# All column transforms in two column tiles of 64, and a quarter of each mix operand copied by GpSimd between the pieces of its zeroing

## The reference

```python
x_ft = jnp.fft.rfftn(_gn(x), axes=(-2, -1))
blk  = jnp.einsum('bimn,hiomn->bhomn', x_ft[:, :, :32, :32], weight)      # 'mix'
xr   = jnp.fft.irfftn(zeros.at[:, :, :32, :32].set(blk), s=(64, 64))
x    = x + jnp.einsum('bchw,oc->bohw', xr, fc_w) + fc_b
g    = _gn(x)
att  = softmax(sigmoid(g.mean((2, 3)) @ ksm_w.T))
kern = clip(ifft2(einsum('bk,koihw->boihw', att, dft_weight)).real)
x    = x + (conv3x3(g, kern) + bias) * fbm_scale
```

## Time and profile before

| what | us |
|---|---|
| median of 3 runs (138.45, 139.57, 140.53) | 139.57 |
| span of the profiled execution | 137.8 |
| TensorE busy in it | 122.5 |
| VectorE, ScalarE, GpSimd busy | 87.8, 70.7, 52.8 |

### The profile page before, as it was taken

How to read it: one execution, slowest core, us unless ns; L and a number is a source line. 1 busy time by engine, 2 the same in 40 slices (tenths; PEclk the granted TensorE clock), 3 DMA queues, 4 the chain that set the end, 5 groups by cost and what they waited for, 6 DMA issues and landing times.

```text
span 137.8 us, 4822 instructions
## 1 busy us (share of the span) xinstructions
PE 122.5 (89%) x2060; PEld 91.8 (67%) x2060; DVE 87.8 (64%) x201; ACT 70.7 (51%) x143; POOL 52.8 (38%) x44
## 2 busy tenths in 40 slices
PE   0799997969997969979999979989999999999970
PEld 0799997869996959979999969873323432223230
DVE  0077696879996743553357685999873789922340
ACT  0468458538965336523317775644998329311100
POOL 7993000009999999999600550130500000000000
PEclk9999999999999999999999999999999999999997
DMA  3999999999500036787876899887989968884477
GB/s 90 268 272 257 233 222 357 302 384 399 204 5 7 0 81 156 171 203 165 181 164 153 172 178 153 180 202 164 168 184 175 211 156 189 195 191 105 104 162 143
DMA packets 71892, 25.17 MB, mean 183 GB/s; under 512 B 67904, under 2 KB 68160, under 8 KB 71872
## 3 DMA queue, kind: packets, MB, share of 16 engines
q1 hardware_dynamic: 70784, 24.62, 77.2%
q10 hardware_dynamic: 1088, 0.26, 0.9%
HBM read 14.38 MB, written 4.19 MB: 135 GB/s over the span
## 4 chain that ended last, share of the span: by engine, by line
PE 86%; issue 5%; DVE 3%; DMA 2%; ACT 0%; SPq 0%
PE slot L1050 27%; PE slot L882 14%; PE slot L963 11%; PE slot L978 8%; PE slot L941 6%; PE slot L952 5%; PE slot L908 3%; PE aggp L1008 3%; PE slot L904 3%; DMA x_buf<-x 2%; PE small L904 1%; PE aggp L904 1%; DVE kern L780 1%; PE aggp L941 1%; PE small L892 1%
## 5 line engine op out<-in xcount | busy, mean ns | idle before, releaser
L1050 PE MATMUL slot<-y_buf,conv_w 128*32 128x512 f32 (+1 forms) x136 | 31.7, 603 | 0.0
L1050 PE MATMUL slot<-w_buf,conv_w 128*32 128x512 f32 (+1 forms) x136 | 31.7, 603 | 0.0
L882 PE MATMUL slot<-cst,x_buf 128*64 128x64 f32 x512 | 19.0, 241 | 5.3 <-DMA x_buf<-x 4.5
L882 PEld LDWEIGHTS slot<-cst,x_buf 128*64 128x64 f32 x512 | 18.4, 154 | 5.6 <-issue 5.5
L821 DVE TENSOR_TENSOR bd_buf<-slot,q_buf 128x512 f32<-128x512 f32 (+1 forms) x17 | 11.0, 670 | 9.3 <-PE slot L1050 9.1
L1050 PEld LDWEIGHTS slot<-y_buf,conv_w 128*32 128x32 f32 x136 | 8.3, 109 | 12.6 <-issue 12.0
L441 POOL TENSOR_TENSOR x_buf<-y_buf 128x1024 f32<-128x1024 f32 x4 | 7.7, 1934 | 22.5 <-DVE y_buf L709 22.5
L978 PE MATMUL slot<-cst,t_buf 128*128 128x128 f32 x128 | 15.5, 278 | 0.8 <-issue 0.8
L978 PEld LDWEIGHTS slot<-cst,t_buf 128*128 128x128 f32 x128 | 14.7, 192 | 1.4 <-issue 1.2
L963 PE MATMUL slot<-cst,r_buf 128*64 128x128 f32 x256 | 14.6, 274 | 0.7 <-ACT r_buf L491 0.7
L613 DVE TENSOR_REDUCE row_sq<-q_buf 128x16 f32<-128x1024 f32 (+1 forms) x9 | 9.8, 1097 | 7.7 <-ACT q_buf L459 7.7
(11 more groups left out here) (128 smaller groups left out, 222.7 us busy)
## 6 DMA issues: line engine op xcount, KB each, us to landing
x_buf<-x SPq DMA_DIRECT2D x16, 256.0 KB, 4.3
w_buf<-w_modes SPq DMA_DIRECT2D x16, 256.0 KB, 5.0
x_buf<-x SPq DMA_DIRECT2D x32, 128.0 KB, 3.1
w_buf<-y_buf SPq DMA_DIRECT2D x16, 256.0 KB, 5.9
out<-bd_buf SPq DMA_DIRECT2D x28, 128.0 KB, 2.8
t_buf<-dft_w SPq DMA_DIRECT2D x4, 288.0 KB, 5.3
t_buf<-x_buf SPq DMA_DIRECT2D x8, 128.0 KB, 2.4
r_buf<-x_buf SPq DMA_DIRECT2D x8, 128.0 KB, 3.4
```

Source lines behind the costliest of these rows:

```text
L882: last = pe.matmul(ps[64 * ri:64 * ri + 64, col:col + 64], x_part(k)[:, i, q, :], const("fwd_h")[:, 64 * ri:64 * ri + 64], start=True, sto ...
L1050: last = pe.matmul(ps[32 * j:32 * j + 32, 32 * u0:32 * u1], cw[r][:, b, k, :], src, start=(k == terms[0][0]), stop=(k == terms[-1][0]))
```

## The change

Three edits. `f2` loses its path with 128 columns: k = 2 and 3 now use two column tiles of 64 like k = 0 and 1. `own_blocks` is gone: VectorE writes block 0 alone, ScalarE blocks 1 and 2. GpSimd copies block 3 from `zn[n]`, in a new function `last_block(n)`: the first before its late zeroing, the second and third between the two zeroings, the fourth between the two halves of the second zeroing, the others behind it and ahead of the 28 steps. `mix` waits for this on `bd_pool` too.

```diff
-        def own_blocks(n):
-            return (0, 1) if n % 2 else (0,)
@@ gpsimd
+            def last_block(n):
+                k, xx = divmod(n, 2)
+                gp.wait_ge(zn_ready, n + 1)
+                nc.gpsimd.tensor_copy(bd[k][96:128, 3, xx], zn[n][96:128]).then_inc(bd_pool, 1)
+                gp.wait_ge(bd_pool, n + 1)
+
+            last_block(0)
             gp.wait_ge(f1_done, 16)
             gp.wait_ge(sq_ready, 9)
             gp.wait_ge(bd_ready, 1)
             nc.gpsimd.memset(x_buf[:, 0:4096], 0.0).then_inc(bd_zero, 1)
             gp.wait_ge(bd_zero, 3)
-            nc.gpsimd.memset(x_buf[:, 4096:8192], 0.0).then_inc(bd_zero, 1)
+            last_block(1)
+            last_block(2)
+            nc.gpsimd.memset(x_buf[:, 4096:6144], 0.0).then_inc(bd_half, 1)
+            gp.wait_ge(bd_half, 1)
+            last_block(3)
+            nc.gpsimd.memset(x_buf[:, 6144:8192], 0.0).then_inc(bd_zero, 1)
             gp.wait_ge(bd_zero, 4)
+            for n in range(4, 8):
+                last_block(n)
@@ scalar, blocks(n)
-                for g in range(len(own_blocks(n)), 4):
+                for g in (1, 2):
@@ vector, operand(n)
-                for g in own_blocks(n):
-                    ps = slice(32 * g, 32 * g + 32)
-                    ins = nc.vector.tensor_tensor(bd[k][ps, g, xx], z[ps], rstd[ps], ALU.mult)
+                ins = nc.vector.tensor_tensor(bd[k][0:32, 0, xx], z[0:32], rstd[0:32], ALU.mult)
@@ tensor, f2_part
-                    if k >= 2:
-                        last = pe.matmul(ps[:, col:col + 64], y_rows[:, b, f:f + 4, :].rearrange("w g c -> w (g c)"),
-                                         const("fwd_w")[:, 0:64], start=True, stop=True)
-                        continue
                     for h in range(2):
                         last = pe.matmul(ps[64 * h:64 * h + 64, col:col + 64],
@@ tensor, mix
                 pe.wait_ge(bd_act, 2 * ml + xx + 1)
+                pe.wait_ge(bd_pool, 2 * ml + xx + 1)
```

More of the change, by code:

```diff
@@ L230, in spectral_then_attention_conv @@
         ones_ready = sem("ones_ready"); s_ready = sem("s_ready"); stat_read = sem("stat_read"); zn_ready = sem("zn_ready"); bd_act = sem("bd_act")
+        bd_pool = sem("bd_pool"); bd_half = sem("bd_half")
         bd_zero = sem("bd_zero"); w_zero = sem("w_zero"); pool = sem("pool_done"); taps_ready = sem("taps_ready")
```

## The result

| | before | changed |
|---|---|---|
| median, us (lowest to highest, runs) | 139.01 (138.01 to 140.61, 6) | 141.50 (140.26 to 142.62, 6) |
| span of the profiled execution, us | 137.8 | 139.6 |
| TensorE, GpSimd busy, us | 122.5, 52.8 | 120.5, 57.5 |

The changed kernel takes 1.0159 times as long, with a 95% interval of 1.0114 to 1.0205: 2.2 us more.

A forecast was written before the change was run, and what follows sets the result against it. The prediction took TensorE's instruction supply to bound the mix stretch: -3.3 us of work, all given back as longer holes, and +1.12 us for mix(3,1) behind the last hole, so 139.57 + 1.1 = 140.7 us, range 138.8 to 142.3.

The forecast's parts named there:

- What bounds the stretch: From 30.17 to 51.17 us, the supply of TensorE's instructions in blocks of 256 sets the pace, not its arithmetic.
- Work off TensorE is given back as holes: In the mix stretch, all 3.3 us of TensorE work saved return as longer holes while it waits for instructions.
- The blocks themselves come when they came before.: In the mix stretch, instruction blocks keep their times, the fifth again at 50.93 us: no loss from later blocks.
- TensorE's own work: In f2(2) and f2(3), matmuls in two column tiles of 64 take 3.3 us less TensorE work.
- GpSimd: Eight new copies of 32x512 at 1.0 us each delay the DFT steps but stay hidden, 0.95 us to spare at i1(3).
- the slower rival: GpSimd's copies and late DFT steps become the bound: 141.7 us at 1.6 us per copy; chance 15%.
- the faster one: In the mix stretch, blocks come early enough for the 3.3 us saving to be real: 138.4 us; chance 12%.
- The third rival: The fifth block comes a microsecond earlier and covers the extra mix(3,1), so time is unchanged at 139.6 us; chance 13%.
- The one term that was in the forecast: At the mix's end, all of mix(3,1) runs behind the last block end, adding 1.12 us.

The follow-up runs named there:

- e1: Kernel before with the transforms of f2(2) and f2(3) in two column tiles, nothing moved to GpSimd: 1.0182 times the kernel before, median 141.49 us after 139.08.
- e2: Changed kernel with f2's 128-column transforms put back, so that only GpSimd's copies of block 3 remain: 1.0022 times the kernel before.
- e3: Kernel before with 32 extra small matmuls (128 more TensorE instructions) ahead of the first transform, where TensorE sits idle: 1.0098 times the kernel before.
- e7: Kernel before with f2(2) in two column tiles too, f2(3) still in 128 columns: 1.0066 times the kernel before.
- e10: Changed kernel with the loads of dft_w and the last quarter of the modes held until the first mix half is done: 1.0111 times the kernel before.
- e11: Kernel before with the loads of dft_w and the last quarter of the modes held until the first mix half is done: 0.9944 times the kernel before.
- e8: Kernel before with one small extra matmul ahead of each of the 32 128-column transforms in f2(2) and f2(3): median 153.47 us.

## Why the prediction was right, and where it was off

The forecast was 140.7 us (+1.1), range 138.8 to 142.3; measured 141.5 (+2.2 by the ratio). The direction and the mechanism were right; the size was half of what was measured. Step by step:

- **What bounds the stretch.** Right. The counts between holes are 253 to 255 for every block now, e1 and e2 put all of the loss on the added instructions' side, and e3 shows it with the transforms untouched.
- **Work off TensorE is given back as holes.** Right: the holes grew from 2.00 to 5.74 us, by more than the work that went. `mix(3,1)` stands behind the last block end, and that block came at 51.21 (forecast 50.93).
- **"The blocks themselves come when they came before."** This is the first term that was mis-sized. The first hole behind 30 us ends 6.54 us after the start of its block in the changed kernel (29.73 to 36.27); I had 5.6 (30.17 to 35.8). The next four came 3.74 us apart on average (to 51.21), as the 3.8 that I had. In e1 these four were 4.24 apart (34.23 to 51.20). The trace has the start of each transfer in the queue "instruction", which narrows it down. For the first block it is 4.31 us behind TensorE's entry into the block before, where the kernel before has 3.22 (30.17 to 33.39), both while loads run. For the later ones it is 1.0 to 1.8 us in the changed kernel and 1.1 to 2.1 in e1. In the kernel before it is 0.5 and 0.3 us at 36.32 and 40.15, where TensorE enters a block without a stop. So the supply is not quite independent of TensorE. A likely reason, which is argued and not shown: before, TensorE's sequencer ran ahead of the matmuls that were queued and asked for the next block early; with an empty queue it asks only when TensorE itself gets there. It does not tell e1 from the changed kernel, and at 47.25 the kernel before took 1.2 us without a stop.
- **The wait of `fc` for VectorE's copy.** Missed. Before, `copy_mixed(3,1)` was over before the last hole had well begun, ahead of the lonely matmul:

```profile
49.40 0.42 DVE L668 COPY q_buf<-slot 128x256 f32<-128x256 f32 x1
```

  Now no hole stands between the mix's end and `fc`, so the copy (52.24) is on the chain and TensorE waits 0.29 us for it.
- **TensorE's own work.** -3.3 forecast, -1.88 measured over the stretch. The granted clock fell behind the hole of 2.46 us: it was 0.50 between 37.30 and 40.60. The 116 mix records from 36.27 on took 2.98 us (25.7 ns, against 17.6 in the earlier trace rows), and the 32 of `f2(3,0)` 1.81, against 1.30 in e1. By these rows the clock took some 1.4 us, an estimate, which is the difference. By itself this need not reach the end, since the next blocks set the pace: in e1, executions with a mean clock of 0.969 and 0.999 took the same time.
- **GpSimd.** Right that it is hidden. The price was 0.61 us and not 1.0. The 1.0 was called the row nearest in size, but that row is L399 with 384 elements and 1.60, not L441 with 1024: the choice of 1.0 had no good reason, and by the nearest row the slower rival's 141.7 would have been the forecast. The DFT steps began at 48.64 (forecast 48.2), since the last copy waits for `zn[7]` and not for the copies before it. The copies of `t` started at 64.32, close to the 64.1 that was forecast, and `i1(3)` was not held. The slower rival fell with it, and so did the faster one: e1 has no GpSimd copies and still no gain.

The third rival (the added half mix is covered after all) fell too. In numbers, of the 2.15 us: 21.48 after 20.76 from the end of the first hole to the last block is +0.72. From there to `fc` it is 1.67 us after 0.24, or +1.43: 0.29 for the copy, and 1.14 for `mix(3,1)`. I had 0, 0 and 1.12. The one term that was in the forecast came out right; the other half of the loss is the later blocks and the copy.

## What to carry to other kernels

When an engine's chain shows holes put down to "issue" with no semaphore behind them, count the instructions between them before you shorten its work: if they come in equal blocks, the stretch is bound by the supply of instructions, and an edit that splits an instruction in two makes it slower even if the engine is then busy for less time. Where instructions are short (the mix halves here ran 256 in 2.2 us, the supply gave 256 in about 4), fewer and wider ones are free up to the point where the holes are gone. And look where a block ends: it cost nearly as much just before a stage as inside the one before, and a hole that goes can put a copy on the chain that was hidden behind it.

## What the runs showed of the hardware that was not expected

- A hole in TensorE's work can be followed by a drop of its granted clock to half, with the matmuls behind the hole 1.5 times as long on average. The window right behind the 2.46 us hole of the changed kernel:

```profile
37.30:40.60 3.30, 3.11 (x88) 2.75 (x81) 1.38 (x2) 0.71 (x2) 3.11 (x4) 0.50 0.07 23
```

  0.50 is the 1.2 GHz level. The traces of e3, e7 and e10 have the same behind holes of 1.56, 2.19 and 3.09 us, from 34.33, 35.90 and 43.86 us on. In e1, with holes of 1.41 and 1.95 us, it did not happen in the profiled execution (clock 0.999), nor in that of e11 with 1.95, so it comes and goes. In e8 the clock fell too, with no such hole in sight (next point), so that a hole is not shown to be the cause.
- Alternating 32-column and 128-column matmuls took 0.60 us per pair, against 0.23 for the 128-column one in a row of its like (e8), and the granted clock was 0.51 between 34 and 46 us of that kernel although TensorE counts as busy all of the time:

```profile
34.00:46.00 12.00, 12.00 (x143) 9.28 (x145) 5.52 (x9) 5.79 (x9) 3.80 (x2) 0.51 0.23 86
```

- A GpSimd copy of 32 x 512 elements took 0.61 us, closer to the 0.46 of the zeroing than to the 0.97 and 1.60 that its two-operand and scaling operations suggested. The Trainium skill's figure for such a size, 0.77 us in "GPSIMD Engine Reference", section 3.1, was nearer than the 1.0 that I took.
